# Row-choice stage of a two-layer sequence kernel: smaller last extremes, twelve-row first ranges, three table pairs made in the loop's drain, one last batch of sixteen

## What is computed

```python
best_cluster = argmax(sign(xf) @ cluster_sigs.T)
tile_idx = argmax(where(in_cluster, sign(xf) @ tile_sigs.T, -inf))     # one slice t of 64 for each row
x_slice = xf[row, 16 * t : 16 * t + 16]
mn, mx = min / max of x_slice over ALL rows that chose the same t      # so nothing can start before the last row is chosen
u = clip((x_slice - mn) / (mx - mn + 1e-8), 0, 1 - 1e-6)
gi = int(u * 16)                                                       # cell of the grid
delta = (bases[t, j, gi] + slopes[t, j, gi] * (u * 16 - gi)) * oscale[t]
out = layernorm(x + (x with delta put in the slice))                    # over all 1024 columns
```

## Time and profile before

| what | us |
|---|---|
| median of 3 runs (lowest, highest) | 1296.49 (1296.23, 1297.9) |
| the profiled execution | 1294.74 |
| its span from the first to the last instruction | 1293.0 |
| DVE busy in the span | 1091.9 (84%) |
| PE busy | 1154.4 (89%) |
| ACT busy | 952.5 (74%) |
| POOL busy | 830.0 (64%) |

### The profile page before, as it was taken

How to read it: one execution, slowest core, us unless ns; L and a number is a source line. 1 busy time by engine, 2 the same in 40 slices (tenths; PEclk the granted TensorE clock), 3 DMA queues, 4 the chain that set the end, 5 groups by cost and what they waited for, 6 DMA issues and landing times. The chain is left out here.

```text
span 1293.0 us, 31770 instructions
## 1 busy us (share of the span) xinstructions
PE 1154.4 (89%) x9346; PEld 733.4 (57%) x9346; DVE 1091.9 (84%) x2532; ACT 952.5 (74%) x1809; POOL 830.0 (64%) x1669
## 2 busy tenths in 40 slices
PE   5799999999999999999999999999999977469730
PEld 4556666666666666666666666666666643333100
DVE  4898888898999899989898999899989883686885
ACT  4657888888888888888888888888888754514781
POOL 3125666777767676767676767676767664524486
PEclk8999999999999999999999999999999987655555
DMA  4012222222222222222222222222222115769998
GB/s 143 33 38 103 104 104 105 104 103 103 103 103 103 103 103 103 103 103 103 103 103 103 103 103 103 103 103 103 103 103 103 71 71 201 264 244 342 376 415 323
DMA packets 63347, 174.86 MB, mean 135 GB/s; under 512 B 11195, under 2 KB 22339, under 8 KB 63302
## 3 DMA queue, kind: packets, MB, share of 16 engines
q1 hardware_dynamic: 52646, 151.43, 31.5%
q10 hardware_dynamic: 5280, 20.97, 4.1%
q0 software_dynamic: 5376, 1.91, 1.0%
HBM read 69.06 MB, written 101.01 MB: 132 GB/s over the span
## 5 line engine op out<-in xcount | busy, mean ns | idle before, releaser
L1052 DVE SCALAR_TENSOR_TENSOR acc<-xT_all,cw_sb,acc 128x256 f32<-128x256 f32 x768 | 353.8, 518 | 6.8 <-ACT acc L751 6.8
L777 ACT ACTIVATE sg<-TX,bet,gam 128x256 f16<-128x256 f32 x256 | 129.8, 557 | 39.9 <-issue 20.1
L1384 POOL TENSOR_TENSOR AT<-AT,Wm 128x128 f32<-128x128 f32 x224 | 114.9, 513 | 40.6 <-DVE AT L1078 24.8
L484 PE MATMUL PR<-xT_all,w_sb 128*128 128x256 f32 x512 | 136.4, 390 | 4.2 <-ACT xT_all L715 4.2
L496 PE MATMUL WK<-w_sb,tS 128*128 128x512 f32 x256 | 137.3, 618 | 0.0
L751 ACT ACTIVATE acc<-xT_all,cb_sb,cw_sb 128x256 f32<-128x256 f32 x256 | 132.5, 592 | 4.8 <-DVE xT_all L1038 2.8
L538 PE MATMUL OB<-th_all,AT 128*128 128x512 f32 x256 | 124.6, 609 | 12.3 <-POOL AT L1384 10.7
L566 PE MATMUL PR<-shT,w_mg_sb 128*64 128x128 f32 x2048 | 128.9, 280 | 6.4 <-ACT shT L760 6.4
L566 PE MATMUL PR<-shT,w_rk_sb 128*64 128x128 f32 x2048 | 125.9, 276 | 0.0
L566 PEld LDWEIGHTS PR<-shT,w_rk_sb 128*64 128x64 f32 x2048 | 110.5, 137 | 25.7 <-issue 25.7
L566 PEld LDWEIGHTS PR<-shT,w_mg_sb 128*64 128x64 f32 x2048 | 113.5, 139 | 18.8 <-issue 12.0
(11 more groups left out here) (236 smaller groups left out, 2698.4 us busy)
## 6 DMA issues: line engine op xcount, KB each, us to landing
xin_all<-in_x SPq DMA_DIRECT2D x32, 1024.0 KB
y_ring<-y_all SPq DMA_DIRECT2D x32, 1024.0 KB, 4.1
y_scratch<-y_all SPq DMA_DIRECT2D x32, 1024.0 KB, 6.1
own<-y_scratch SPq DMA_DIRECT2D x5, 2048.0 KB, 16.3
rows<-y_scratch SPq DMA_DIRECT2D x4, 2048.0 KB, 12.5
out<-rows ACTq DMA_DIRECT2D x3, 2048.0 KB, 8.5
out<-own ACTq DMA_DIRECT2D x3, 2048.0 KB, 16.5
RX<-RE SPq DMA_DIRECT2D x128, 32.2 KB
```

What stands on the lines that cost most here:

```text
L484: i = pe.matmul(PR[:, 0:T], w0_sb[:, blk, :], xT[b][:, blk, HIST:HIST + T], start=(blk == 0), stop=(blk == NB - 1))
L777: nc.scalar.activation(sg[:, blk, :], TX[:, (blk % 2) * T:(blk % 2 + 1) * T], ACT.Sign, scale=gam[:, blk:blk + 1], bias=bet[:, blk:blk + 1 ...
L1052: v.scalar_tensor_tensor(acc[:, blk, :], xT[b][:, blk, i:i + T], cw_sb[:, blk, i:i + 1], acc[:, blk, :], ALU.mult, ALU.add).then_inc(e_con ...
L1384: q.tensor_tensor(late, late, Wm[:, :, l, :].rearrange("p c (n h) -> p c n h", h=h), ALU.add)\
```

## The change

It touches only the drain of part one and part two.

- `extremes` gets the ends 16, 40, 60, 62 and 64: the call in the drain takes columns 40 to 60, and after the pipeline follow 60 to 62 and 62 to 64.
- PE makes the first three table pairs (`early_tables`, twelve matmuls of 512 columns) in the drain, between the fifth and the sixth block of one-hot transposes. For this the three Z buffers are PSUM tensors that live through both parts (`OB`, `WKB`, `TS`, which part one uses for other things), and the counter of finished pairs is `z_rd`.
- The three bf16 parts of the extremes lie in one 128 x 4 tile `t3q`, so that `ranges` has one matmul with four output columns for each column instead of two with two; DVE adds the two halves afterwards (one more instruction).
- `RANGES` are 0 to 12, 12 to 36 and 36 to 64; `BATCHES` are 4, 8, 12, 12, 12 and 16.
- In `cells` the cell comes from one conversion to a byte instead of two additions of a large constant, and two temporaries are bytes.
- `DIRECT` is 11: one unit more is stored by ACT and patched by POOL's indirect stores, one less by DVE's `put`.
- The correction of the last batch comes ahead of all `put`s instead of ahead of the last four.

```diff
-    EXT_ENDS = (16, 40, 56, 64)
+    EXT_ENDS = (16, 40, 60, 62, 64)
+    EARLY = 3
+        OB, WKB, TS = (whole.enter_context(nc.psum_tensor(n, [P, 2 * HALF], F32)) for n in ("OB", "WKB", "TS"))
+        z_rd = whole.enter_context(nc.semaphore("z_rd"))
...
+                def early_tables():
+                    pe.wait_ge(s_ohe, 1)
+                    for t, (e, z) in enumerate(((e_y[1], OB), (e_S[1], WKB), (e_km, TS))):
+                        done(pe, e, NG - 1)
+                        for j in range(2):
+                            cols = slice(j * HALF, (j + 1) * HALF)
+                            pe.matmul(z[:, cols], ohT[:, 2 * t + j, :], t2s01[:], start=True, stop=False)
+                            i = pe.matmul(z[:, cols], ohT[0:NT, 2 * t + j, :], t2s2[:], start=False, stop=True)
+                        i.then_inc(z_rd, 1)
                 for f in range(NC // 8 - 1):
+                    if f == 5:
+                        early_tables()
...
-                            extremes(40, 56)
+                            extremes(40, 60)
...
                 pipeline(dve, step, 4)
-                extremes(56, NC)
+                extremes(60, 62)
+                extremes(62, NC)
...
-            BATCHES = (4, 8, 12, 12, 12, 12, 4)
+            BATCHES = (4, 8, 12, 12, 12, 16)
-            RANGES = ((0, 4), (4, 12), (12, 36), (36, NC))
+            RANGES = ((0, 12), (12, 36), (36, NC))
-            DIRECT = 10
+            DIRECT = 11
...
-                BEHIND = (0, 1, 3, 4, 6, 7, DIRECT)
+                BEHIND = (0, 1, 3, 4, 6, DIRECT)
...
                     for n in range(lo, hi):
-                        pe.matmul(QB[:, n * 2:(n + 1) * 2], ohT[:, n, :], t3s01[:], start=True, stop=False)
-                        i = pe.matmul(QB[:, n * 2:(n + 1) * 2], ohT[0:NT, n, :], t3s2[:], start=False, stop=True)
+                        i = pe.matmul(QB[:, n * 4:(n + 1) * 4], ohT[:, n, :], t3q[:], start=True, stop=True)
...
                 ranges(*RANGES[0])
-                tables(0)
-                tables(1)
+                last_turned()
+                for t in range(EARLY, 6):
+                    tables(t)
                 ranges(*RANGES[1])
-                last_turned()
-                for s in range(2, 6):
-                    tables(s)
+                for t in range(6, 12):
+                    tables(t)
                 ranges(*RANGES[2])
...
+                v.memset(t3q[:], 0.0).then_inc(p_v, 1)
...
-                    v.tensor_copy(rng3[:, lo:hi, :], QB[:, lo * 2:hi * 2].rearrange("p (n k) -> p n k", k=2)).then_inc(p_rc, 1)
+                    q = QB[:, lo * 4:hi * 4].rearrange("p (n k) -> p n k", k=4)
+                    link(v.tensor_copy(rng3[:, lo:hi, :], q[:, :, 0:2]))
+                    v.tensor_tensor(rng3[:, lo:hi, :], rng3[:, lo:hi, :], q[:, :, 2:4], ALU.add).then_inc(p_rc, 1)
...
-                    x, g, t, c = (a[:, lo:hi, :] for a in (xfs, outs, w_o, cell))
+                    x, g, t, c = (a[:, lo:hi, :] for a in (xfs, bits[0], bits[1], cell))
...
-                    link(v.tensor_scalar(g, x, MAGIC, None, ALU.add))
-                    link(v.tensor_scalar(g, g, -MAGIC, None, ALU.add))
+                    link(v.tensor_copy(g, x))
...
                 dve.wait_ge(p_in, 1)
-                dve.wait_ge(p_out, len(BATCHES) - 1)
-                for n in range(4 * DIRECT, starts[-2]):
-                    put(n)
                 corrections(len(BATCHES) - 1)
-                dve.wait_ge(p_out, len(BATCHES))
-                for n in range(starts[-2], NC):
+                for n in range(4 * DIRECT, NC):
+                    if n in (4 * DIRECT, starts[-2]):
+                        dve.wait_ge(p_out, batch_of(n) + 1)
                     put(n)
```

More of the change, by code:

```diff
@@ L226, in build @@
             st = sb("st", [P, 7, CPG])
-            TX = psum("TX", [P, HALF])
+            TX, SC1 = TS[:, 0:HALF], TS[:, HALF:2 * HALF]
             with ExitStack() as loop_only:
@@ L232, in build @@
             OT = [psum(f"OT{i}", [P, 8, P], BF16) for i in range(2)]
-            SC = [SC0, psum("SC1", [P, HALF])]
-            WK = [psum(f"WK{i}", [P, HALF]) for i in range(2)]
-            OB = psum("OB", [P, 2 * HALF])
+            SC = [SC0, SC1]
+            WK = [WKB[:, h * HALF:(h + 1) * HALF] for h in range(2)]
             s_cw = sem("s_cw")
@@ L1542, in build @@
             o_off = sb("o_off", [P, NC])
+            m_sq = o_off
             in_row = sb("in_row", [P, NC - 4 * DIRECT, NT], U8)
             own = [sb(f"own{i}", [P, 4, D]) for i in range(OWN)]
-            Z = [psum(f"Z{i}", [P, 2 * HALF]) for i in range(3)]
+            Z = [OB, WKB, TS]
             OT2 = psum("OT2", [P, 8, P], BF16)
@@ L1550, in build @@
             p_oh, p_ohT, p_ohTe, p_extT, p_t3, p_r3, p_rc = (sem(n) for n in ("p_oh", "p_ohT", "p_ohTe", "p_extT", "p_t3", "p_r3", "p_rc"))
-            p_v, p_z, p_zf, p_gi, p_in, p_put = (sem(n) for n in ("p_v", "p_z", "p_zf", "p_gi", "p_in", "p_put"))
+            p_v, p_zf, p_gi, p_in, p_put = (sem(n) for n in ("p_v", "p_zf", "p_gi", "p_in", "p_put"))
             p_sum, p_m, p_coef, p_row, p_out, p_sc, p_i = (sem(n) for n in ("p_sum", "p_m", "p_coef", "p_row", "p_out", "p_sc", "p_i"))
@@ L1683, in _ @@
                 ranges(*RANGES[0])
-                tables(0)
-                tables(1)
+                last_turned()
+                for t in range(EARLY, 6):
+                    tables(t)
                 ranges(*RANGES[1])
-                last_turned()
-                for s in range(2, 6):
-                    tables(s)
+                for t in range(6, 12):
+                    tables(t)
                 ranges(*RANGES[2])
-                for s in range(6, 12):
-                    tables(s)
-                ranges(*RANGES[3])
-                for s in range(12, PAIRS):
-                    tables(s)
+                for t in range(12, PAIRS):
+                    tables(t)
             @block.scalar
@@ L1717, in _ @@
                 v = nc.vector
-                count = [0]
+                count = [1]
                 def link(ins):
@@ L1788, in chosen @@
                                 if i == 3:
-                                    dve.wait_ge(p_z, s0 + h + 1)
+                                    dve.wait_ge(z_rd, s0 + h + 1)
                                 else:
```

18 lines of the change are left out of this document (7 added, 11 removed).

## The result

| what | before | after |
|---|---|---|
| median of 7 runs each (lowest, highest), us | 1296.49 (1293.28, 1298.71) | 1286.46 (1285.2, 1291.9) |
| the profiled execution | 1294.74 | 1288.54 |
| its span | 1293.0 | 1286.8 |

The ratio is 0.9932 with a 95% interval of [0.9916, 0.9949]: 8.8 us less than before, between 6.6 and 10.9 (the two medians lie 10.0 apart). The forecast was 1293.5 us, a gain of 3.0, with a range down to 1290.5.

A forecast was written before the change was run, and what follows sets the result against it. The prediction took the tail to be paced by transferred bytes: first store -0.6, holes -2.1, mixing -0.6, indirect stores +0.3 gave -3.0 us, so the median goes from 1296.49 to 1293.5, range 1290.5 to 1297.0.

The forecast's parts named there:

- (a): Last extremes, before part two: the two-column last call saves 2.4 us, POOL's gather stalls cost +0.8 (0 to +1.7).
- (b): Early tables in part one's drain: twelve matmuls take 3.2 us and hide behind DVE; boundary -1.6 us.
- (c): Head of part two: `in_row` -0.45, first ranges +0.5, cells +1.2 us; together +1.0 (+0.6 to +1.5).
- after the first store: Part two from the first store on: holes -2.1, mixing -0.6, four more indirect stores +0.3 us.
- cover of 0.9: End of part one: the early tables, with ACT's copy, finish at 1133.4, before DVE at 1134.3, 0.9 us to spare.
- early tables at 1.2 GHz: Rival, drain: table matmuls take 6.5 us, boundary +0.8 instead of -1.6, so -0.6 us in all, 1295.9; chance 0.18.
- four more cost at most 0.55: Head of part two: first ranges go from 8 matmuls to 12, taken as +0.5 us (+0.4 to +0.55).
- The next ranges cost half the matmuls: Part two's later ranges: the wait of 0.92 goes, and most of the 3.41 before batch 3.
- holes: DMA engines' idle stretches up to 1214: earlier stores fill them, -2.1 us (-1.0 to -2.1).
- mixing: Transfers up to 1214: a longer queue may mix loads among slow stores, -0.6 us (0 to -2.6).
- better mixing: Rival: the longer queue brings 344 GB/s up to 420, end 5 to 6 us earlier, 1291.0; chance 0.18.
- the rival close by: Rival, tail: POOL's 20 indirect stores behind the last coefficients become the end, up to 1301.4; chance 0.07.

The follow-up runs named there:

- e4: The kernel after with the old ends of the extremes (16, 40, 56, 64): 1290.67 us, ratio 0.9952 to the kernel before.
- e9: The kernel after with the second matmul of each table padded with zeros to full height: 1284.78 us, ratio 0.9913 to the kernel before.
- e7: The kernel after, with SP issuing each store from unit 11 on only when the one before has landed: 1291.35 us, one run.
- e12: The kernel after with the old last batches (12 and 4), `DIRECT` 10 and the old order of puts: 1286.58 us, ratio 0.9927 to the kernel before.
- e5: The kernel before with only the new tail (last batch of sixteen, `DIRECT` 11, last correction ahead of all puts): 1297.22 us, ratio 1.0016.
- e8: The kernel after with two matmuls per column in the ranges, both of full height: 1286.79 us, ratio 0.9934 to the kernel before.
- e1: The kernel after with the old two matmuls per column in the ranges (128 and 64 rows): 1291.3 us, ratio 0.9963 to the kernel before.

## Why the prediction was wrong in size and right in sign

Counted from the mark, predicted against found, in us:

| step | predicted | found |
|---|---|---|
| boundary (a), (b) | -1.6 | -1.44 |
| head (c), to the first predicated copy | +1.0 | +0.04 |
| from there to the first store | 0 | -0.52 |
| after the first store | -2.4 | -6.14 |
| sum | -3.0 | -8.06 |

**(a) Last extremes: right.** The two-column call takes 3.03 (3.0 predicted), and the 60 to 62 call lies in idleness. The wait of 1.60 at `key_u` is gone, as foreseen. The gathers do suffer. Timeline of POOL in after, the slices of the last but one group, then of the last:

```profile
1112.66 2.17 POOL L1468 DMA_INDIRECT gbs<-gb_table,gix  x1 [0.30 <-issue]
...
1116.39 2.04 POOL L1468 DMA_INDIRECT gbs<-gb_table,gix  x1 [0.30 <-issue]
...
1126.70 0.96 POOL L1468 DMA_INDIRECT gbs<-gb_table,gix  x1 [0.30 <-issue]
...
1138.01 2.31 POOL L1653 CAST in_row<-oh 128x1280 uint8<-128x1280 bf16 x1
```

The twenty-column call stretches two gathers to 2.17 and 2.04 (1.77 before), whereas the two-column call beside the last group's leaves them at 0.94 to 1.01. By e4 the net price is 0.48 us. Against before, DVE starts the last call 0.91 later from the mark (36.02 and 35.11), close to the 0.8 taken; where the other 0.43 comes from isn't shown.

**(b) Early tables: hidden, as said, but at another price, and worth nothing.** The pitch in the drain is 0.32, not 0.27: at the level of 2.4 GHz (PEclk 1.00 from 1129 to 1133) a table matmul is 0.216, and the change of height adds 0.10 (e9). Half of 0.54 was the wrong scaling, because of the 0.54 only the part without the 0.11 scales with the clock. The twelve take 3.85 us instead of 3.2. ACT's last copy ends 0.16 us ahead of DVE:

```profile
1134.10 2.00 ACT L970 ACTIVATE ohT<-OT 128x1024 bf16<-128x1024 bf16 x2 [1.78 <-PE OT L712]
```

It ends at 1136.10 and DVE's last instruction of part one at 1136.26. The cover of 0.9 that the prediction counted on was thus 0.16. The rival "early tables at 1.2 GHz" is out: the clock was up, after transposes and little else. This is against what the Trainium skill (TensorE: Matmul & The Clock Gate, "Part 4: PE-mode transpose") says of transposes. The rival's premise that tables don't raise the clock isn't general either: in e9 it rose after eight of them (see the last section).

**(c) Head: the step that failed first, "four more cost at most 0.55".** `in_row` is 2.31 as predicted (2.28). The cells of twelve, from the copy of the ranges to the first predicated copy, take 4.55 (4.6). Wrong was the +0.5 for four more matmuls at the old pitch. It took the 1.10 that DVE waited for eight matmuls as an upper bound for what twelve of any kind cost, and never asked what made them so slow. Twelve took 0.48 us, and DVE's wait fell from 1.10 to 0.57. The term was -0.5 instead of +0.5, and this is the whole of the miss in the head. The other -0.5 up to the first store: DVE doesn't wait 0.21 for the second pair (a saving that the prediction had booked in the head), and POOL's moments ran in 3.06 instead of 3.28 us beside predicated copies instead of cells.

**After the first store: the mechanism right, the size wrong by nearly 4 us.** "The next ranges cost half the matmuls" is where the sum broke. The third and fourth call took 5.7 and 6.6 us; halved they would still have been 2.8 and 3.3. They became 0.80 and 0.91. With that the waits of 0.92 and 3.41 vanish wholly. From DVE's first row of part two, the first store of batch 3 leaves 9.4 us sooner, where 7 to 8 were forecast, and the second store 3.9 sooner, where about 3 were. All bytes after the first store would take 115.7 us at 420 GB/s; before lost 13.8 us beyond that and after 7.4. The forecast had 2.7 of these 6.4 (holes 2.1, mixing 0.6). The rival "better mixing", with -5 to -6 and 1291.0, came nearest. Its reason is not shown: e7 shows the gaps as such, but why before also moves few GB/s at a nearly full share (344 at 0.96), and after 411 in the same stretch, stays open. It goes with stores that arrive sooner; whether the deeper queue itself or the loads among them make it, no run tells apart.

**The tail: right in sum, with the rival close by.** The last batch of sixteen and the 20 indirect stores cost little or nothing in the kernel after only because everything ahead of them is faster (e12). Put into the kernel before they make POOL the end (e5), which the prediction gave 7 in 100, deciding from a mean of 2.1 us. It had the coefficients at 1244, 149 us after the mark; in e5 they came after 157, and there a mean of 1.76 was enough. What protected the kernel is that the ranges became cheap, which the prediction didn't know. It also asked only that POOL stay below the transfers, and counted nothing behind them. The DRAIN behind POOL's last landing is in both kernels, so it hardly touches the sum: 0.32 us for four more indirect stores. But it means that POOL's last landing set the end of the span in both, and that faster batches do more than "lengthen the queue": in e9 they are worth 4.1 us from the mark to the end of the span.

**Other signs.** The first DVE row of part two was to be near 1134.8; with the mark 1.85 later it is 1136.83, 39.62 after the mark (39.4 predicted). The copies of the later ranges wait for nothing, but "no wait at the second and third batch" was not met, as waits of 1.59 for table pairs are left in both. The DMA share is 0.95 from 1172 to 1175 and 1.02 to 1.03 from 1193 to 1280, as foreseen. POOL issues its last indirect store before the transfers end, as foreseen, but its landing is what the end of the span waits for.

The parts don't add up. Counted from DVE's first row of part two to the end of the span, so that the boundary stays out, the cheap matmuls alone give -4.2, the ranges of twelve -0.6 and the tail +0.8. With -1.4 of the boundary that is -5.4, and the change gives -8.1. That the tail costs less when the batches come sooner is one part of the missing 2.7 (e5 against e12); how the rest divides is not shown.

## What to carry to other kernels

Before pricing matmuls by number, look at the pitch of their starts against the pitch of others of the same kind, and at the shapes in the weight-load rows: where weights of 128 and 64 rows alternate, padding the short one with zeros may be free and faster, for small and large matmuls alike. Where transfers pace the end, an earlier start counts only as far as the work behind it keeps the rate up; so look for the first stretch in which the rate falls, and speed up what feeds it. Compare the end of the span with the end of the last transfer: a time between them that changes from kernel to kernel, as here from 0.8 to 4.9 us, is work to be hidden, as by the faster batches of e9. A part that is slower alone may be free in company, so test an edit of the tail in the kernel it is meant for.

## What the runs showed of the hardware that was not expected

- **Weight loads of equal height overlap, those that alternate between 128 and 64 rows don't.** In the ranges each lasts 0.10 us either way, but they start every 0.027 us (e8: 128 and 128 rows) or every 0.117 us (e1: 128 and 64 rows), at PEclk 0.50. Behind 512-column matmuls the same change costs 0.11 us at PEclk 0.50 and 0.10 at 1.00 (e9). The Trainium skill (TensorE: Matmul & The Clock Gate, "Step-by-step: what each phase is for") says that the next weights are pulled ahead of running matmuls if their row groups don't conflict or the background buffer is used, and that the row count doesn't matter for the load's timing. The traces agree as to the length of one load, and e9 shows the pull ahead by 0.43 us. They don't agree for alternating heights, where the load starts with its own matmul and the row count sets the pitch.
- **An indirect store issued by POOL takes 2.07 us instead of 0.96 while DVE puts rows** (e5, nine in a row at the one, then nine at the other), and gathers take 2.17 and 2.04 beside a long call of `extremes`, but 0.94 to 1.01 beside one whose instructions last 0.42 us or less. The long call's instructions last up to 1.49 us. A gather that ran beside instructions of the same call of 0.49 us and less took 0.95 (after, 1115.14). The puts and the long call share that DVE's single instructions are long, which is what the runs have to say on the cause.
- **POOL has a DRAIN of 3.33 us behind 40 indirect stores and of 3.65 behind 44** at the end of the program, the same in every trace of either number. It starts 0.2 us after the last of them has landed. Whether it depends on their number alone no run tells.
- **One 2 MB store at a time has a gap of about 2 us** at each hand-over, with 393 to 414 GB/s between the gaps (e7).
- **The clock of PE didn't rise under the densest work.** Windows of PE, first of after and then of e9 (length, busy, PEclk, DMA share, GB/s):

```profile
1129.00:1133.00 4.00, 3.75 (x15) 1.00 0.07 6
1150.00:1155.00 5.00, 4.92 (x10) 0.50 0.79 323
```

```profile
1150.00:1154.00 4.00, 3.30 (x8) 0.50 1.02 419
1154.00:1159.00 5.00, 4.17 (x40) 1.00 0.12 46
```

After, ten table matmuls in a row ran at 0.50 with PE 4.92 of 5 us busy; in e9, eight at 0.50 were followed by 5 us at 1.00. The runs don't tell what makes the difference.
